# Directional convolution on one core: loop written out, a third buffer of sums, statistics over two tiles

## The reference

```python
v = group_norm(x, groups=32, eps=1e-5)
h = gelu(depthwise_conv3x3(v, dw_weight))
maps = (einsum('bchw,oc->bohw', h, pw_weight) + pw_bias).reshape(B, 8, C, H, W)
out = x + sum(maps[:, i] * (roll(v, (dy, dx)) - v) for i, (dx, dy) in enumerate(OFFSETS8))
```

## Time and profile before

| | |
|---|---|
| median of 3 runs | 2328.58 us (2322.09 to 2330.8) |
| the profiled execution | 2324.94 us, its span 2323.3 us |
| TensorE, VectorE busy | 2204.9 us (95%), 2073.9 us (89%) |
| GpSimd, ScalarE busy | 1985.9 us (85%), 1824.0 us (79%) |
| matmuls | 10752 |

### The profile page before, as it was taken

The page is one execution under the profiler, slowest core; times in us unless marked ns, Lnnn a source line. Parts: engine busy times, 40 slices in busy tenths (PEclk is TensorE's granted clock), DMA queues, the critical chain, the costliest instruction groups (busy, mean ns, idle before and its releaser), DMA issues.

```text
span 2323.3 us, 34233 instructions
## 1 busy us (share of the span) xinstructions
PE 2204.9 (95%) x10752; PEld 2025.1 (87%) x10752; DVE 2073.9 (89%) x2210; ACT 1824.0 (79%) x2764; POOL 1985.9 (85%) x862
## 2 busy tenths in 40 slices
PE   1999999999999999999999999999999999999997
PEld 1989889888889988898888998889898898998996
DVE  7998989989899898999989999898998999999983
ACT  5968879787787877879788797877878778797774
POOL 5788898888888888898888888889888898998986
PEclk9999999999999999999999999999999999999998
DMA  5235263443625426163352644426353361642433
GB/s 171 64 63 121 48 113 88 87 96 58 144 46 104 96 49 152 32 120 93 60 127 40 112 96 80 105 49 127 71 103 86 60 151 33 112 97 38 96 49 55
DMA packets 47200, 202.82 MB, mean 87 GB/s; under 512 B 3088, under 2 KB 7184, under 8 KB 45712
## 3 DMA queue, kind: packets, MB, share of 16 engines
q0 software_dynamic: 30528, 95.43, 25.2%
q1 hardware_dynamic: 16464, 104.88, 17.3%
HBM read 104.88 MB, written 146.80 MB: 108 GB/s over the span
## 4 chain that ended last, share of the span: by engine, by line
PE 72%; issue 10%; DVE 8%; ACT 6%; DMA 2%; POOL 1%; DVEq 0%; ACTq 0%; POOLq 0%
PE psum L846 72%; ACT psum L566 3%; DVE psum L724 3%; DMA out<-acc 2%; DVE psum L715 1%; ACT squares_out L445 1%; DVE acc L692 1%; POOL acc L350 1%; DVE dev_t L633 1%; ACT xn L515 1%; DVE products L670 1%; DVE dev_t L636 1%; ACT hid L551 1%; DVE acc L670 0%; DMA fields<-x 0%
## 5 line engine op out<-in xcount | busy, mean ns | idle before, releaser
L566 ACT ACTIVATE psum<-psum,bias,rstd 128x448 f32<-128x448 f32 x1792 | 1210.7, 701 | 384.9 <-PE psum L846 373.5
L846 PE MATMUL psum<-hhi,w_hi 128*128 128x448 f32 x3584 | 1318.5, 368 | 100.8 <-ACT hhi L556 47.9
L350 POOL TENSOR_TENSOR acc<-acc,products 128x896 f32<-128x896 f32 x336 | 1213.3, 3611 | 223.2 <-DVE products L670 219.2
L846 PE MATMUL psum<-hhi,w_lo 128*128 128x448 f32 x3584 | 1311.1, 366 | 0.0
L846 PE MATMUL psum<-hlo,w_hi 128*128 128x448 f32 x3584 | 1019.9, 366 | 0.3 <-POOL hlo L323 0.3
L724 DVE SCALAR_TENSOR_TENSOR psum<-xn,dw_f,psum 128x896 f32<-128x896 f32 x768 | 882.3, 1149 | 4.0
L846 PEld LDWEIGHTS psum<-hhi,w_hi 128*128 128x128 f32 x3584 | 677.1, 189 | 175.5 <-DVE acc L692 57.3
L846 PEld LDWEIGHTS psum<-hlo,w_hi 128*128 128x128 f32 x3584 | 676.3, 189 | 53.3 <-POOL hlo L323 0.9
L846 PEld LDWEIGHTS psum<-hhi,w_lo 128*128 128x128 f32 x3584 | 677.2, 189 | 51.7
L670 DVE TENSOR_TENSOR products<-psum,fields 128x896 f32<-128x896 f32 x560 | 607.7, 1085 | 44.0 <-ACT psum L566 38.9
L670 DVE TENSOR_TENSOR acc<-psum,fields 128x896 f32<-128x896 f32 x224 | 243.3, 1089 | 168.1 <-ACT psum L566 142.5
(11 more groups left out here) (65 smaller groups left out, 474.3 us busy)
## 6 DMA issues: line engine op xcount, KB each, us to landing
out<-acc POOLq DMA_DIRECT2D x96, 896.0 KB, 7.9
out<-x SPq DMA_DIRECT2D x16, 3136.0 KB, 12.0
xpad<-x SPq DMA_DIRECT2D x30, 1568.0 KB, 14.3
out<-acc POOLq DMA_DIRECT2D x16, 448.0 KB, 5.6
fields<-x SPq DMA_DIRECT2D x4, 784.0 KB, 7.1
xpad<-pw_t SPq DMA_DIRECT2D x1, 2048.0 KB, 12.5
spare<-zeros POOLq DMA_DIRECT2D x2, 0.5 KB, 5.4
dw_f<-dw SPq DMA_DIRECT2D x1, 9.0 KB, 8.3
```

What stands on the lines that cost most here:

```text
L350: nc.gpsimd.tensor_tensor(a, a, p, ALU.add).then_inc(added_s, 1)
L566: nc.scalar.activation(m, m, ACT.Identity, bias=bias[ip][:, g, d:d + 1], scale=rstd[ip][:, g:g + 1]).then_inc(biased_s, 1)
L846: last = nc.tensor.matmul(maps(q)[:, side, :], w[:, kk, col:col + P], h_part(h, t, nl, kk), start=s == 0, stop=s == len(steps) - 1)
```

## The change

- Every engine's `Fori` loop is replaced by a plain Python loop over 8 bodies, so that the program is written out.
- `acc` gets a third buffer, of half size, for an image's last tile. The two others alternate over the three pairs of an image.
- The ring of fields has three tiles instead of four; in 14 tiles 6 instead of 4 are fresh.
- `group_stats` starts in tile 2 behind product 6 and ends in tile 3: five steps in each. ScalarE's measuring steps stand a little earlier.
- GpSimd's sends are issued later, between other operations, and `differences` is split in two calls.
- The first image is copied by GpSimd alone; two small DMAs at the start are gone.
- The sums of the very last tile are formed by VectorE in `last_tile`, and SyncE stores them.

```diff
-    FIELD_AT = (0, 1, 2, 3, 1, 2, 3)
-    FIELD_FRESH = (0, 4)
+    FIELD_AT = (0, 1, 2, 0, 1, 2, 0, 2, 0, 1, 2, 0, 1, 2)
+    FIELD_FRESH = (0, 3, 6, 7, 8, 11)
...
-        acc = [sb(f"acc{i}", [P, HALVES, 2, 2, PX]) for i in range(2)]
+        sums_t = sb("acc", [P, 2 * PAIR_SUMS + PAIR_SUMS // 2])
...
-        MEASURE_AT = ((0, 3), (0, 5), (0, 6), (1, 3), (1, 4), (1, 5), (1, 6), (2, 3), (2, 4), (2, 5), (2, 6), (2, 7))
-        STATS_TILE = 3
+        MEASURE_AT = ((0, 3), (0, 4), (0, 5), (0, 6), (1, 3), (1, 4), (1, 5), (1, 6), (2, 2), (2, 3), (2, 4), (2, 5))
+        STATS_TILE, SCALES_TILE = 2, 3
...
-            with engine.Fori(0, BODIES - 1) as i:
-                body(i * STEPS, i * 2, False)
-            body((BODIES - 1) * STEPS, (BODIES - 1) * 2, True)
+            for i in range(BODIES):
+                body(i * STEPS, i * 2, i == BODIES - 1)
...
@@ GpSimd, a tile
                     if more(1):
-                        differences(b0, nl + 1)
+                        differences(b0, nl + 1, 0)
+                    if t == 0 and n:
+                        send_folded(n - 1)
+                    elif t and t % 2 == 0:
+                        send_left(n - 1)
+                    if more(1):
+                        differences(b0, nl + 1, 1)
                     if more(2):
                         split_h(n0, nl + 2)
-                    add_pair(n0, nl, 1)
+                    if more(1):
+                        add_pair(n0, nl, 1)
...
+                    if more(1):
+                        add_pair(n0, nl, 2)
                     if t and t % 2 == 0:
-                        send_right(b0, nl - 1)
-                    add_pair(n0, nl, 2)
-                    add_pair(n0, nl, 3)
-                    if t == TILES - 1:
-                        send_single(n0, b0, nl)
-                    elif t % 2:
-                        send_left(n0, b0, nl)
+                        send_right(n - 1)
+                    if more(1):
+                        add_pair(n0, nl, 3)
+                        if t == TILES - 1:
+                            fold(n)
...
@@ ScalarE, first image
-                for c in range(SLICES):
-                    act.wait_ge(first_in[1][c], 16)
-                    nc.scalar.copy(rows_of(0, 1, c), first[:, 1, c]).then_inc(x_in[0][1], 16 // SLICES)
...
@@ VectorE, the very last tile
+            def last_tile(n0, nl):
...
+                for u in range(HALVES, UNITS):
+                    g = u % HALVES
+                    product(n0, nl, u, maps(nl * UNITS + u)).then_inc(scaled_s, 1)
...
+                    nc.vector.tensor_tensor(a[:, g], maps(nl * UNITS + u), a[:, g], ALU.add).then_inc(prod_s, 1)
...
@@ VectorE, a tile, behind product 4 (the steps behind taps 1 and 2 and behind product 2 are gone as well)
                     kept_product(n0, nl, 4)
+                    tap_next()
+                    kept_product(n0, nl, 5)
+                    tap_next()
+                    kept_product(n0, nl, 6)
+                    if t == STATS_TILE and not (last and par):
+                        stats = iter(group_stats(b0 + par + 1))
                     stats_next()
                     tap_next()
                     stats_next()
-                    kept_product(n0, nl, 5)
                     tap_next()
-                    kept_product(n0, nl, 6)
-                    tap_next()
-                    tap_next()
+                    stats_next()
                     kept_product(n0, nl, 7)
                     tap_next()
+                    stats_next()
+                    stats_next()
```

More of the change, by code:

```diff
@@ L160, in step_of, with place_of, sums_of @@
             return ip, s, s % 2, 2 * (s // 2)
[L162 to L176, removed]
+        def place_of(n):
+            b, t = divmod(n, TILES)
+            if t == TILES - 1:
+                return b, 2, b, t, 1
+            k = b * TPAIRS + t // 2
+            return b, k % 2, k // 2, t - t % 2, 2
+        def sums_of(n):
+            return acc[place_of(n)[1]][:, :, :, n % TILES - place_of(n)[3], :]
         def h_part(h, t, nl, kk):
@@ L285, in body @@
                         load_image(b0 + par + 2, par)
-            loop(sp, body)
+            run(body)
+            sp.wait_ge(laid[1], 16 * BODIES)
+            for g in range(HALVES):
+                sp.wait_ge(final_s, g + 1)
+                sp.dma_start(out_dst[B - 1, :, g, (TILES - 1) * PX:TILES * PX],
+                             products[:, g, 0, :]).then_inc(last_sent[g], 16)
+            for g in range(HALVES):
+                sp.wait_ge(last_sent[g], 16)
             for i in range(2):
-                sp.wait_ge(all_sent[i], 16 * BODIES * TPAIRS + SENT0)
+                sp.wait_ge(all_sent[i], 16 * (B * TPAIRS // 2))
+            sp.wait_ge(all_sent[2], 16 * (B - 1))
         @block.gpsimd
@@ L356, in send @@
                 pool.sem_inc(sends, 1)
[L357 to L367, removed]
@@ new lines, in send_left, with send_right, fold @@
+            def send_left(n):
+                if n % TILES == 1:
+                    pool.wait_ge(laid[n // TILES % 2], 16 * (n // TILES // 2 + 1))
+                pool.wait_ge(added_s, (n + 1) * ADDS + ADD0)
+                send(n, 0, left_sent)
+            def send_right(n):
+                b, buf, used, t, width = place_of(n)
+                pool.wait_ge(left_sent[buf], 16 * (used + 1))
+                send(n, 1, all_sent)
+            def fold(n):
+                pool.wait_ge(added_s, (n + 1) * ADDS + ADD0)
+                a = sums_of(n)
@@ L391, in _ @@
             pool.wait_ge(first_s, FIRST)
-            pool.wait_ge(x_in[0][1], 16)
-            pool.wait_ge(measure, MEASURES)
-            differences(0, 0)
+            for axis in range(2):
+                differences(0, 0, axis)
             split_h(0, 0)
@@ L601, in body @@
                             wrap(b0 + par + 1, 1 - par)
-            loop(act, body)
+            run(body)
         @block.vector
@@ L855, in body @@
                         make_maps(n0, nl, u)
-            loop(pe, body)
+            run(body)
 def kernel(x, L0_conv_dw_weight, L0_conv_pw_weight, L0_conv_pw_bias):
```

136 lines of the change are left out of this document (81 added, 55 removed).

## The result

The changed kernel takes 2356.1 us (median, 2353.0 to 2358.4) beside 2329.2 for the one before on the same chips: ratio 1.0123, interval 1.0097 to 1.0148. It is slower by 27 us. The profiled execution took 2353.0 us, 28.1 more than that of before.

A forecast was written before the change was run, and what follows sets the result against it. TensorE sets the time, losing mostly behind VectorE's second add L692. From 2324.9 us: -2.1 head, -18 loop and buffer, -5 last tile, +58 statistics, +6 clock gave 2364 us; 8 in 10 range 2265 to 2378.

The forecast's parts named there:

- Head: At the start, ScalarE's two half-image copies go to GpSimd, so VectorE's statistics wait less: -2.1 us (0 to -3).
- Loop and third buffer: Loop seams and waits for the buffer being sent go, winning TensorE's waits there: -18 us (-10 to -20).
- Smaller ring: About 1 us more GpSimd work on fields per two images, within its waiting time: nothing directly.
- Statistics: Over tiles 2 and 3, small VectorE operations wait for GpSimd: +3.6 or +4.2 us an image, +58 us in all.
- clock: Longer TensorE pauses bring the lower clock, costing 1.5 us each, behind 4 more of 15 statistics: +6 us.
- K: End of product 7 in tile 2, 680.4 before; forecast to come 0.8 us later, with the add ending at K + 14.35.
- step 5: L636, behind product 7 in tile 2: finds GpSimd's next fields operation under way and ends at K + 6.0.
- Rival one: Step 5 slips into a gap between GpSimd operations; statistics cost 27 us, time 2329, no change; chance 0.15.
- Rival two: Step 4 doesn't wait for GpSimd's add, the statistics' load is halved: 2272 us, or 2250; chance 0.24.
- step 4: L633, one tap behind product 7 in tile 2: waits for GpSimd's whole third add, ending at K + 4.3.
- Rival three: ScalarE's back-to-back sums and squares in tiles 0 and 1 make products late, another 1 us an image: 2379; chance 0.08.
- Last tile: At the end, VectorE forms the final sums and SyncE sends half the bytes without accumulation: -5 us (-3 to -9).

The follow-up runs named there:

- Undoing the edits: Changed kernel with the statistics' ten steps back in tile 3 and ScalarE's measuring steps where they stood before: 2293.3 us, ratio 0.9855 to the kernel before.
- quiet places: Changed kernel with statistics steps 3 to 7 in a row before product 7 and 8 to 10 behind the second add: 2286.8 us, 0.982 of the kernel before.
- other forms: Changed kernel with subtraction, square and scaling of the statistics replaced by transposes in the same places, so output differs: 2273.9 us, ratio 0.9792 to the kernel before.
- steps 4 and 5 early: Changed kernel with these two statistics operations moved from behind product 7 and its tap to in front of product 7: 2304.5 us, ratio 0.9901 to the kernel before.
- both causes away with old places: Changed kernel with 64 unused bytes ahead of the weights and the statistics in their old places in tile 3: 2284.3 us, ratio 0.9813 to the kernel before.

## Why the prediction was right, point by point

**What bounds it.** TensorE, held at the statistics by L692's place in VectorE's order: right; after the change it is held a second time, at first product 0, as forecast.

**Head, -2.1.** -2.5: the first matmul's wait went from 47.9 to 45.4.

**Loop and third buffer, -18.** Right in kind, too small: outside tiles 3 and 4 all waits behind seams and buffers are gone, and with them the slower first steps and the small delays around them, some 26 us. Wrong was to hold both edits for needed. The loop alone does most of it (53.1 us of waits in the middle become 37.3). The count of executed instructions, which I held to stay, fell from 34233 to 28668.

**Smaller ring, nothing.** Wrong in a way that the argument couldn't see. No loss shows in GpSimd's part (busy 1979.9 us after 1985.9), but with the larger `acc` the ring moved the weights by 64 bytes, and this costs some 16 us by the run with the weights back (7 to 8 us in the kernel before). Over all undisturbed steps of the trace the mean is 0.2039 us instead of 0.2019, which makes 21 us. This is the one term that was missing.

**Statistics, +58, and clock, +6.** The mechanism is shown step by step: K + 4.3, 6.0, 9.8 and 14.35 were forecast, K + 4.2, 5.9, 9.7 and 14.05 came. The odd images' fields are fresh and hold step 5 for 2.0 us instead of 1.63, as forecast. Rival one is out: step 5 never slips in; its least time in a body is 1.63 us. Rival two is out: step 4 waits for the whole add in 15 of 15. Rival three isn't seen: TensorE's waits behind L690 and L712 all lie at the statistics and in the tile after, but for 0.2 us at the start.

The size was somewhat too large. From tile 3's first matmul to unit 5 it is 3.0 us more in the even images and 3.6 in the odd ones, where 3.6 and 4.2 were forecast: **+49**, not +58. Undoing the edits gave 63 us, but that isn't this term, for it is measured against the old places within the changed kernel and the sum against the kernel before. What was mis-sized is mainly K's own delay. I took 0.8 us; tile 3's first matmul and K lie at 677.11 and 680.39 before, at 681.91 and 685.46 after:

```profile
677.11 0.36 PE L846 MATMUL psum<-hhi,w_hi 128*128 128x448 f32 x1
```
```profile
681.91 0.36 PE L898 MATMUL psum<-hhi,w_hi 128*128 128x448 f32 x1
```

That is 3.55 instead of 3.28, 0.27 later. Product 5 did wait for its bias, 0.59 us at 678.89, but VectorE had come to it earlier (product 4 starts 5.77 us ahead of the tile's first matmul instead of 5.40), and product 6 then starts only 0.09 us later than before. The add ended at K + 14.05, not 14.35.

The clock's +6 was wrong in its effect, though more stretches came, as forecast. Between the first and the last matmul the clock stands at the lower level for 10 stretches of 3.4 us before and for 14 after (two of them joined). I priced each by its slow matmuls. But after the change all of them begin in the wait for first product 0 or behind it and end ahead of unit 5, where TensorE would have waited for the add, so they cost nothing on top. Before, all ten stand at unit 5 or up to 1.1 us behind it; there they delay, but no image with one waits in tile 4, and three of the five without one do, for 0.6 us. From unit 5 to the end of tile 4 it is 27.9 us before and 28.1 after, no more than the slower pace gives. So the clock's term is about nothing. The two means of 0.989 don't show this, for they take in the idle end behind the last matmul, longer before and mostly at the lower level. The third figure from the end is the granted clock, first before, then after:

```profile
2306.20:2323.20 17.00, 0.00 (x0) 0.00 (x0) 1.09 (x1) 0.52 (x1) 8.03 (x4) 0.57 0.31 48
```
```profile
2345.00:2351.10 6.10, 0.00 (x0) 0.00 (x0) 3.63 (x5) 0.39 (x1) 0.00 (x0) 0.64 0.30 94
```

**Last tile, -5.** The end behind the last matmul shrank from 17.3 to 6.5 us, less 1.2 us of waiting for L742: -9.6. The size was off because I priced SyncE's store by the 8.3 us that GpSimd's DMA and the end had taken together; it lands in 1.9, and from the last sum to the end it is 2.4 us instead of the 6.5 taken:

```profile
out<-products SPq DMA_DIRECT2D x2, 224.0 KB, 1.9
```
```profile
2348.18 0.63 DVE L745 TENSOR_TENSOR products<-acc 128x448 f32<-128x448 f32 x1
```
```profile
2344.10 0.56 PE L898 MATMUL psum<-hlo,w_hi 128*128 128x448 f32 x2
```

**The sum.** 2364 forecast, 2356 measured, 2353.0 in the profiled execution, on which the terms can be laid: head -2.5, loop and buffer about -26, statistics +49, clock about 0, last tile -9.6, the matmuls' pace outside these tiles about +19. The four terms after the head each came out 5 to 9 us lower than forecast, and the pace, which wasn't in the sum, took back most of it. The mechanism of the term that decides was right; that the total came so close is partly luck.

## What to carry to other kernels

A tiny VectorE operation with two SBUF operands, or a scaling, isn't tiny beside GpSimd: put it where GpSimd is waiting or issuing, or give it another form, and look for its price in the duration of the operation, not in idle time. Compare the time between two fixed points of a stage, not the waits in it, for slow matmuls can stand in the place of a wait. Before a loop or a buffer is blamed for a wait, look whether the engine that sets the end waits for it at all. And when a tile's size changes, compare the pace of undisturbed matmuls before and after, for other tiles have moved.

## What the runs showed of the hardware that I had not expected

- 64 bytes in the weights' address (in the kernel before tried as 960 the other way, the same modulo 1024) change the matmul's undisturbed step: 452 or 442 in 90 us (about 0.200 and 0.2035 us), the same way in two kernels.
- With the weights in their first place the step can change within one execution from 0.200 to 0.207 us and back at a stall, and stays for hundreds of matmuls. It is in this count of slow steps that executions of like kernels differ most (700 to 4,000 of 10,752).
- A step of 2 elements (L670, two SBUF inputs and a constant) waits for GpSimd as the 32-element ones do: 1.02 us in the median where it met an add, 0.15 where not.
- Stretches of 3.4 us at the lower clock (1.2 GHz) between the first and the last matmul, beside TensorE's longest wait in the middle: none in six executions with 1.1 to 1.4 us (all with quiet places or other forms); 1, 5 and 7 with 2.3 us (statistics in old places, steps 4 and 5 early, kernel before with the weights moved); 6, 9 and 10 with 2.5 us (both causes away with old places, loop alone, kernel before); 14 with 3.4 us (changed kernel); 21 with 3.9 us (the same with the weights back). The length of a wait alone doesn't settle it.
- A stretch at the lower clock costs nothing where the engine that is waited for sets the time: in the changed kernel all 14 lie between two waits for VectorE, and the second wait is 0.4 to 0.9 us with one and 2.0 us without.
